# Output products of three expert heads from slot tiles sorted by output expert, and interleaved adds on VectorE

## What is computed

```python
gate_v = _get_sel_gate(x, sel_v_w, rs)      # [B,S,H,E], two of eight experts are not zero
gate_o = _get_sel_gate(x, sel_o_w, rs)
xv = jnp.einsum('bsd,hedp->bshep', x, v_w.reshape(H, E, D, P))
v = jnp.einsum('bshep,bshe->bhsp', xv, gate_v)
att = jax.nn.softmax(jnp.einsum('bhqp,bhkp->bhqk', q, k) * SCALE, axis=-1)
ctx = jnp.einsum('bhqk,bhkp->bqhp', att, v)
weighted = ctx[:, :, :, None, :] * gate_o[..., None]
out = jnp.einsum('bshep,hepd->bsd', weighted, o_w.reshape(H, E, P, D))
```

## Time and profile before

| what | value |
|---|---|
| median of 3 runs | 2006.86 us |
| the profiled execution | 2006.01 us |
| its span, first to last instruction | 2004.2 us |
| PE busy in the span | 1829.3 us (91%) |
| DVE / ACT / POOL busy | 1511.5 / 972.1 / 897.0 us |
| mean granted TensorE clock | 0.953 |

### The profile page before, as it was taken

One profiled execution on the slowest core, in us unless ns is written; L12 is line 12 of the kernel. 1 busy time (PEld: TensorE's weight loads), 2 busy tenths in 40 slices (PEclk: granted clock), 3 DMA queues, 4 the chain that ended last, 5 costly groups with the idle time before them and its releaser, 6 DMA issues. The chain is left out here.

```text
span 2004.2 us, 32861 instructions
## 1 busy us (share of the span) xinstructions
PE 1829.3 (91%) x9946; PEld 1012.3 (51%) x9946; DVE 1511.5 (75%) x4406; ACT 972.1 (49%) x2260; POOL 897.0 (45%) x1307
## 2 busy tenths in 40 slices
PE   6499997699989948987999999999999999999998
PEld 4233333455556633334566666644455555555543
DVE  6588886677747757997576677468877788888998
ACT  3267884476744415421577777633333333333332
POOL 1547771266623311111366677654544455434440
PEclk9689998799989969998899999999999999999999
DMA  8552224333530039911654555211313242432211
GB/s 285 143 126 39 38 23 76 110 104 85 128 89 22 22 92 179 200 49 51 179 169 150 154 162 159 87 62 45 96 61 97 90 129 83 138 103 77 63 32 29
DMA packets 240450, 201.86 MB, mean 101 GB/s; under 512 B 26868, under 2 KB 222874, under 8 KB 239640
## 3 DMA queue, kind: packets, MB, share of 16 engines
q1 hardware_dynamic: 222472, 171.36, 33.1%
q0 software_dynamic: 17376, 28.29, 5.3%
q10 hardware_dynamic: 432, 0.10, 0.0%
HBM read 116.80 MB, written 82.89 MB: 100 GB/s over the span
## 5 line engine op out<-in xcount | busy, mean ns | idle before, releaser
L2863 DVE SCALAR_TENSOR_TENSOR x<-f_m,f_gs,x 128x128 f32<-128x128 f32 x1024 | 353.3, 348 | 78.7 <-PE f_m L2688 52.7
L515 DVE TENSOR_REDUCE a_nmax<-a_s 128x1 f32<-128x512 f32 (+3 forms) x512 | 276.4, 585 | 80.4 <-PE a_s L321 26.5
L2236 POOL TENSOR_SCALAR a_lg<-a_lg,a_rinv 128x256 f32<-128x256 f32 (+1 forms) x256 | 225.3, 897 | 156.9 <-DVE a_rinv L2273 156.4
L2688 PE MATMUL f_m<-f_wo,f_oT 128*128 128x512 f32 x512 | 261.4, 595 | 1.8 <-DVE x L2863 1.0
L2636 POOL DMA_INDIRECT f_yg<-yslot,slot x160 | 151.6, 947 | 199.5 <-PE f_s L2722 98.1
L432 ACT ACTIVATE a_pT<-a_st 128x512 f32<-128x512 f32 (+3 forms) x512 | 226.9, 520 | 18.6 <-PE a_st L344 7.0
L318 PE MATMUL a_s<-t_kp,t_qp 96*128 96x512 bf16 (+3 forms) x512 | 163.7, 354 | 12.5 <-DVEq L499 12.0
L341 PE MATMUL a_st<-t_qp,t_kp 99*128 99x512 bf16 (+3 forms) x512 | 160.7, 349 | 2.2 <-ACT a_pT L432 1.5
L2816 ACT COPY f_pT<-f_t 128x512 f32<-128x512 f32 x128 | 75.2, 587 | 146.5 <-PE f_t L2730 121.4
L2863 DVE SCALAR_TENSOR_TENSOR f_val<-f_m,gate,f_val 128x128 f32<-128x128 f32 x336 | 113.4, 344 | 40.8 <-PE f_m L2688 27.1
L2688 PEld LDWEIGHTS f_m<-f_wo,f_oT 128*128 128x128 f32 x512 | 91.2, 190 | 97.9 <-issue 82.0
(11 more groups left out here) (429 smaller groups left out, 3816.7 us busy)
## 6 DMA issues: line engine op xcount, KB each, us to landing
a_band<-band SPq DMA_DIRECT2D x64, 512.0 KB, 4.3
band<-s_hole SPq DMA_DIRECT2D x16, 1032.0 KB
band<-a_rows SPq DMA_DIRECT2D x64, 256.0 KB, 3.7
yslot<-f_ys SPq DMA_DIRECT2D x45, 256.0 KB
f_xs<-spare_rows SPq DMA_DIRECT2D x9, 832.0 KB
w_gate_up<-f_wgu_in SPq DMA_DIRECT2D x4, 1536.0 KB, 14.7
t_qp<-parts SPq DMA_DIRECT2D x192, 32.0 KB
t_kp<-parts SPq DMA_DIRECT2D x192, 32.0 KB
```

Of the source, the lines that this page charges most:

```text
L515: v.tensor_reduce(nmax[:, h % 4, qt:qt + 1], s_ps[(b * H * QT + u) % R][:, 0:n], AX.X, ALU.max, negate=True)\
L2236: last = pool.tensor_scalar(lg[:, g % 2, half, p, c0:c0 + n], lg[:, g % 2, half, p, c0:c0 + n], rinv[:, g % 2, p, qt:qt + 1], None, ALU.mult)
L2688: pe.matmul(ps[:, :], left, w, start=True, stop=True).then_inc(full, 1)
L2863: ins = v.scalar_tensor_tensor(out, ps[:, e * P:(e + 1) * P], gate, out, ALU.mult, ALU.add)
```

## The change

The outputs of heads 0 to 2 (`SPARSE_O`) are made in the sorted way too, from a second routing of the tokens by output expert. Their context rows are turned the other way (`values` makes tokens by width), scattered by POOL into two more DRAM lists, loaded, transposed (`xo`), multiplied with one expert a tile (`zo`), stored, fetched by POOL and added into `x` by DVE (`add_out`, `add_rest`). POOL may have up to 5 indirect DMAs a unit. In heads whose v is sorted, the y fills come two a pair, of two token tiles, so that DVE's additions alternate between them.

```diff
-    CUTS = (0, 5, 10, 15, GATE)
-    CHAINS = {2: (0, 0), 6: (0, 1), 20: (1, 0), 24: (1, 1)}
...
+    CUTS = (0, 7, 14, GATE)
+    CHAINS = {2: (0, 0), 5: (0, 1), 16: (1, 0), 19: (1, 1)}
+    ROUTE_LEN = 1 + NT + 13 + ROUTES
...
+    ROUTE_STEPS = ((0, 9), (9, 1 + NT), None, (20, 24), (24, 29), (29, 31), (31, 33), (33, 33 + ROUTES))
+    ROUTE_AT = (8, 22)
+    COUNT_AT = tuple(g + 2 for g in ROUTE_AT)
...
-    H, E, CHUNK, FILLS, RING, EACH = 8, 8, TILES // 3, -(-TILES // 4), 3, 3
+    H, E, CHUNK, FILLS, RING, EACH = 8, 8, TILES // 3, -(-TILES // 4), 3, 5
...
-                     and not (f[0] == "v" and f[1] // B in SPARSE)]
+                     and f[1] // B not in (SPARSE if f[0] == "v" else SPARSE_O)]
                     for i in range(2)]
     pairs[LAST] = [[("y", G - 1, i), ("y", G - 1, i + 2)] for i in (0, 1, 4, 5)]
+    for g in range(G - 1):
+        of = range(QT * (g + 1) + 3, QT * (g + 2) + 3)
+        if g // B not in SPARSE_O and all(f[0] == "y" for u in of for pair in pairs[u] for f in pair):
+            for u, i in zip(of, (0, 1, 4, 5)):
+                pairs[u] = [[("y", g, i), ("y", g, i + 2)], []]
...
+    def opens_o(h):
+
+        return QT * B * h + 26
...
-                moves[QT * (g - 1) + i].append(("gather", g, i))
+                moves[QT * (g - 1) + i // 2].append(("gather", g, i))
+    adds = {u: [] for u in range(LAST + 1)}
+
+    def put(u, move):
+
+        while 2 * len(moves[u]) + 2 > EACH:
+            u += 1
+        moves[u].append(move)
+        return u
+
+    for h in SPARSE_O:
+        for g in range(B * h, B * h + B):
+            for i in range(QT):
+                put(QT * (g + 1) + 2, ("scatter_o", g, i))
+    ends = [0, 0]
+    for h in SPARSE_O:
+        for g in range(B * h, B * h + B):
+            u = max(opens_o(h) + QT * QT + 6, ends[g % 2] + 1)
+            u = max(put(u, ("gather_o", g, i)) for i in range(QT)) + 4
...
+                elif kind == "xs_o":
+                    n = nth_o(i)
+                    for s in sent_o:
+                        sp.wait_ge(s, 16 * NT * (n + 1))
...
+            def scatter_o(g, i):
+                h, b = g // B, g % B
+                n = nth_o(h)
+                if i == 0:
+                    pool.wait_ge(o_read, g + 1)
...
+                for c in range(2):
+                    pool.indirect_dma_start(out_rows[n % 2], place_o(c, b * QT + i, h), oT[:, g % 2, i * P:(i + 1) * P], None)\
+                        .then_inc(sent_o[g % 2], 16)
...
+                if g // B in SPARSE_O:
+                    for qt in range(QT):
+                        at = slice(qt * P, (qt + 1) * P)
+                        for kt in range(QT):
+                            last = pe.matmul(o_ps[:, at], pT[:, g % 2, kt, at], val[:, g % 3, kt, :],
+                                             start=(kt == 0), stop=(kt == QT - 1))
...
+                    if (g - 2) // B in SPARSE_O:
+                        act.wait_ge(sent_o[g % 2], 16 * 2 * QT * (turn_o(g - 2) // 2 + 1))
                     act.copy(oT[:, g % 2, :], o_ps[:, :]).then_inc(o_read, 1)
...
-            spare_rows = [nc.dram_tensor(f"spare_rows{i}", (TILES * P, P), F32, kind="Internal").ap() for i in range(2)]
+            spare_rows = [nc.dram_tensor(f"spare_rows{i}", (TILES * P, P), F32, kind="Internal").ap() for i in range(4)]
```

More of the change, by code:

```diff
@@ L1878, in relative_heads @@
     H, DH, C, W, NB = 16, 64, 8, 257, 6
-    TRIPLES = [range(h, min(h + 3, 8)) for h in range(SPARSE[0], 8, 3)]
-    ROUTES = 2 * len(TRIPLES) + 1
+    TRIPLES = ((range(3, 6), range(6, 8)), (range(0, 3), range(3, 5)))
+    ROUTES = 2 * 2 + 2
     G = B * C
@@ L2207, in _ @@
                     exponentials(g, 0, 1)
+                if odds_at(g) is not None:
+                    s, half = odds_at(g)
+                    act.wait_ge(stepped, (CHAIN_START[s, half] + BEST))
+                    act.activation(k.share[:, s, :, half * HF:(half + 1) * HF, :], top[:, :, :, :], ACT.Exp, scale=-1.0)\
+                        .then_inc(odds, 1)
                 if g >= 1:
@@ L2504, in index, with nth_o, index_o, stores @@
         return FILLS * nth(h) + j
-    def stores(h, j):
-        return sum(1 for g in SPARSE for i in range(FILLS) if (nth(h) - nth(g)) % 2 == 0
-                   and index(g, i) <= index(h, j) and (index(g, i) - index(h, j)) % RING == 0)
+    def nth_o(h):
+        return SPARSE_O.index(h)
+    def index_o(h, j):
+        return FILLS * nth_o(h) + j
+    def stores(heads, h, j):
+        i, n = heads.index(h), FILLS * heads.index(h) + j
+        return sum(1 for a in range(len(heads)) for f in range(FILLS) if (i - a) % 2 == 0
+                   and FILLS * a + f <= n and (FILLS * a + f - n) % RING == 0)
     def turn_of(g):
         return B * nth(g // B) + g % B
+    def turn_o(g):
+        return B * nth_o(g // B) + g % B
     plain = [g for g in range(G) if g // B not in SPARSE]
@@ L2519, in switch_heads @@
             for i in range(QT):
-                moves[QT * (g - 1) + i].append(("gather", g, i))
+                moves[QT * (g - 1) + i // 2].append(("gather", g, i))
[14 more added lines that the diff above has]
+            u = max(put(u, ("gather_o", g, i)) for i in range(QT)) + 4
+            for i in range(QT):
+                while adds[u]:
+                    u += 1
+                adds[u].append((g, i))
+            ends[g % 2] = u
     waiting = [(h, i, c) for h in SPARSE for i in range(NT) for c in range(2)]
@@ L2528, in switch_heads @@
         assert max(u for u in moves for m in moves[u] if m[0:2] == ("scatter", h)) < opens(h)
+    for h in SPARSE_O:
+        assert max(u for u in moves for m in moves[u] if m[0] == "scatter_o" and m[1] // B == h) < opens_o(h)
     def tiles_of(j):
@@ L2541, in switch_heads @@
         fold = ph.sb("fold", [P, H, P])
-        wo = ph.sb("wo", [P, 2, 2, 512])
+        wo = ph.sb("wo", [P, 3, 1024])
+        yslot_o = [nc.dram_tensor(f"yslot_o{i}", (TILES * P, P), F32, kind="Internal").ap() for i in range(len(SPARSE_O))]
         gs = ph.sb("gs", [P, 2, QT, E])
@@ L2560, in switch_heads @@
         m_free = [ph.sem(f"m_free{i}") for i in range(4)]
-        wo_in, got = ([ph.sem(f"{n}{i}") for i in range(2)] for n in ("wo_in", "got"))
+        wo_in = [ph.sem(f"wo_in{i}") for i in range(3)]
+        got, got_o, sent_o = ([ph.sem(f"{n}{i}") for i in range(2)] for n in ("got", "got_o", "sent_o"))
+        xs_o_in = [ph.sem(f"xs_o_in{i}") for i in range(3)]
+        kept_o = [[ph.sem(f"kept_o{i}{j}") for j in range(RING)] for i in range(2)]
+        shared, halved, added = ph.sem("shared"), ph.sem("halved"), ph.sem("added")
         sent = [ph.sem(f"sent{i}") for i in range(3)]
@@ L2897, in scaled_gates, with scaled @@
                 v.wait_ge(rinv_ready, g + 1)
+                if g // B in SPARSE_O:
+                    share = k.share[:, 1, :, g % B * QT:(g % B + 1) * QT, g // B]
+                    v.tensor_tensor(share, share, bc(rinv[:, g % 2, :].unsqueeze(1), [P, 2, QT]), ALU.mult).then_inc(shared, 1)
+                    return
                 v.tensor_tensor(gs[:, g % 2, :, :], gates[:, g % B * QT:(g % B + 1) * QT, 1, g // B, :],
                                 bc(rinv[:, g % 2, :].unsqueeze(2), [P, QT, E]), ALU.mult).then_inc(gs_ready, 1)
+            def scaled(g):
+                return sum(1 for i in range(g + 1) if i // B not in SPARSE_O)
             v.wait_ge(k.f3_in, 16 * len(k.f3))
@@ L3136, in program @@
         Phase.retire(nc)
-        layer3(nc, k, d, band, (rows, *spare_rows), out)
+        layer3(nc, k, d, band, (rows, *spare_rows[0:2]), spare_rows[2:], out)
 def laid_out(a):
```

243 lines of the change are left out of this document (167 added, 76 removed).

## The result

The changed kernel takes **2177.11 us** (median of 4 runs, 2175.31 to 2181.96), the kernel before 2006.1 (4 runs): a ratio of 1.0859, 95% interval 1.0832 to 1.0886. It is slower, as forecast, but by 171 us instead of 23, far outside the range. The profiled execution took 2181.96 us at a span of 2180.2.

A forecast was written before the change was run, and what follows sets the result against it. PE bounds the kernel before; in the changed one POOL's queue holds group 17's `combine` until 1725.8 us. With 298.6 us remaining that gives 2024.4, with attention's +4 a span of 2028.4, forecast 2030 us; range 2012 to 2056.

The forecast's parts named there:

- PE's part: TensorE work in the expert phase: fewer y fills against added transposes and products, net -42.6 us.
- The attention part: Before the expert phase: second counts, second routing chain and longer gate chains, +4 us, bounds 0 and +14.
- POOL's price: Each indirect DMA of 128 rows occupies POOL for 1.26 us, for scatters as for fetches.
- the path: Up to group 17: its last fetch, the 324th DMA, holds `combine` and so PE 19.4 us past its old time.
- three places where stalls were to build up: ACT's copy of `f_oT`, SP's loads of sorted output rows, `combine` in groups 12 to 17; not added up.
- After group 17: From its `combine` to the end: 297.8 us before, +5.8 for late fills, -5 for additions, so 298.6 us.
- Rival B: After group 17 POOL itself waits and groups pay a 2.8 us landing: about 2056 us (2045 to 2075), chance 0.13.
- DVE's additions: Additions into `x` alternate between two banks: 0.24 to 0.27 us each instead of 0.38; -5 us taken.
- The clock: TensorE's clock may sag up to group 17 while PE idles; costed at nothing, hidden while POOL is the bound.
- Rival A: POOL's 0.30 us between DMAs vanishes when they queue up, PE stays the bound: 1957 us (1950 to 1970), chance 0.07.
- Rival C: Time within 0.3% of before (6 us either way), waits recovered and a slightly cheaper DMA: 2003 us, chance 0.06.

The follow-up runs named there:

- runs with rests: Changed kernel with one or two memsets of 128x1024 on POOL after every fourth indirect DMA: 2110.56 us with one, 2229.04 us with two.
- the pairs alone: Kernel before with only the new pairing of y fills, no second routing or sorted outputs, POOL's list unchanged: 1991.04 us, ratio 0.9929.

## Why the prediction was wrong

- **PE's part** (-42.6 us): no run measures it apart, and nothing speaks against it. A product of 128x512 still takes 0.86 us (the queries, 1326.23 to 1327.09 above). But nothing of it shows: up to `combine` of group 17 PE is idle 124.5 of 527.4 us, where some 67 were expected.
- **The attention part** (+4): measured -0.5. PE's busy time in its window rose by 1.4 us and DVE's by 20, and both found room. The term stood too high; 0 was the end to take, since DVE had 120 us free.
- **POOL's price** was right, 1.26 us a DMA, and so was the order: the 324th is the last fetch of group 17. As a path the sum shows only in the changed kernel's runs with rests, and purely in that with two. POOL never waits there, 324 DMAs (408) and 80 pairs of memsets at 1.83 us each (147) take the 555 us from 1311.7 to 1867.0 that its trace shows, and `combine` follows 2.6 us after the issue, where 2.8 was taken. That 2.8 was luck: the landings of the earlier trace rows are those of SP's eight loads `f_yg<-yall` of the earlier layer, not of POOL's fetches. The sum also counts 324 intervals up to the start of the 324th DMA where there are 323, which is 1.3 us.
- **The step that failed** is the path: that PE is held by `combine` of group 17 and `combine` by its last fetch, "issued at 1723.0 if POOL never waits". POOL does wait: it issued that DMA at 1817.60, 503.4 us after its first one instead of 408.3. And nobody waited for it: `combine` ran 22.7 us after the issue, at 1840.26, with DVE busy just before it and idle before that for a late signal of PE.

```profile
1817.60 0.95 POOL L2745 DMA_INDIRECT f_yg<-yslot,slot  x1 [0.30 <-issue]
...
1839.65 0.69 DVE L3040 COPY f_ys_o<-f_m 128x512 f32<-128x512 f32 x1 [3.42 <-remote]
```

  So it is in all twenty sorted groups (9 to 28 us from the last fetch to `combine`, DVE never idle ahead of it), and no wait of PE, ACT, DVE or POOL in the phase is put down to a DMA: none of the three places where stalls were to build up did so. In numbers, POOL's own delay of 95 us and the 20 us between landing and `combine` come on top of the forecast 19.4 and make up the 134.3. The prediction treated the 408 us as a pure occupation of POOL, beside which the others work on or wait for its data. The runs put in its place: an unbroken run of POOL's DMAs holds back PE's signals, so ACT, DVE and then PE come late, and POOL, which waits for PE's units and ACT's copies, comes late with them. The same rows of before showed it in small: a run of twelve DMAs at 1314.7 to 1328.6, PE's transposes that end at 1325.1 and their copy at 1330.3, and the five lines shown above.
- **After group 17** (298.6 us): measured 339.9. The late signals go on, since value and output fetches stand eight and ten in a row; PE is idle 35.5 us there, before 10.9. **Rival B** has no part in it that shows: no `combine` waits for a landing, and POOL waits for DVE's `combine` no longer than before (waits of POOL, after from 1840.3 us to the end, before from 1706.4):

```profile
POOL f_yg L2745 <- DVE f_val L3066: 43.1, 10, 10.7
...
POOL f_yg L2636 <- DVE f_val L2891: 46.0, 9, 5.7
```

- **DVE's additions** in turn: eight in 2.15 us (0.27 each) in head 7, within the 0.24 to 0.27 given.

```profile
2132.81 2.15 DVE L3011 SCALAR_TENSOR_TENSOR x<-f_m,f_gs,x 128x128 f32<-128x128 f32 x8
```

  What they are worth was under-sized: 5 of 13 us were taken, the pairs alone brought 14 by the ratio.
- **The clock**: 0.80 to 0.89 in heads 0 to 3, where PE waited; it was named, and counted as hidden. How much of the loss it makes was not measured apart; an estimate of PE's extra busy time, 707.3 us against 674.2 - 42.6, is some 76 us, and what it shares with the waits is not known.
- **Rival A** (1957 us) is out: the DMAs of the changed kernel keep their distance. The sentence of the Trainium skill behind it ("DMA: Bandwidth & Descriptors", on the SWDGE path), that many descriptors can be given out before their cost shows, does not hold for these DMAs of 128 rows: 25 in a row take 1.26 us each. **Rival C** is out too. The direction was right, but not for the reason given: POOL's queue is not what the others waited for in this kernel. The case that decided, a signal that is late without anyone being late, was not among the rivals.

## What to carry to other kernels

Count how many indirect DMAs GpSimd issues without a break, not only how many there are and when their data is due: in this kernel runs of up to six cost next to nothing, eight with rests between them some 20 us and twelve over 100, with the same DMAs. Spread them, or put a short piece of other work after every fourth; a pause there can make a kernel faster, though with 512 DMAs in one stretch one such piece left 121 late signals, and two cost more than they gave back. When all engines of a profile are half idle, look for waits put down to nobody or to a DMA of long ago, and compare the end of the instruction that should have released them with the start of the one that waited.

## What was not expected of the hardware

- TensorE's semaphores rose as late as 17.7 us after the end of the matmul that raises them (the copy at 1348.05), while GpSimd issued indirect DMAs 1.26 us apart; no late one of ScalarE or VectorE was found. They began some 10 us into a run and ended up to 4 us after it (1345.6 to 1349.5). In the meantime they come through singly, 3 to 7 us apart: ACT and DVE were released at 1328.4, 1332.0, 1334.7, 1338.2, 1341.0 and 1348.0.
- It is the DMAs and not a busy GpSimd: 160 memsets between them took the delay away. It does not depend on the direction: scatters in head 0 and fetches in head 6 do it.
- Why a DMA that GpSimd issues delays a signal of TensorE, and how long a pause has to be when the load lasts for hundreds of us (0.97 us after every four was enough for groups of twelve, and not for 512 DMAs in one stretch), stays open; no run here shows the path.
